# Sparse graph attention: sources projected ahead of targets, adjacency loaded from the start, gathers in memory of their own

## The reference

```python
hs = layer_norm(x); ht = layer_norm(h_target)            # masked by nodemask
q = (ht @ Wq + bq) / sqrt(32); k = hs @ Wk + bk; v = hs @ Wv + bv
logits = where(adj != 0, q . k, -1e30); probs = softmax(logits)     # per head
ht = layer_norm(ht + probs @ v @ Wo + bo); ff = gelu(ht @ W1) @ W2
out = layernorm(x + ht + ff)
```

## Time and profile before

| | us |
|---|---|
| median of 3 runs | 367.64 (366.29 to 369.21) |
| the profiled execution | 366.63 |
| its span | 364.8 |
| PE / DVE / ACT / POOL busy | 247.2 / 233.4 / 157.8 / 191.1 |
| mean granted clock of PE, of 1 | 0.867 |

### The profile page before, as it was taken

The page is one execution under the profiler, slowest core; times in us unless marked ns, Lnnn a source line. Parts: engine busy times, 40 slices in busy tenths (PEclk is TensorE's granted clock), DMA queues, the critical chain, the costliest instruction groups (busy, mean ns, idle before and its releaser), DMA issues. The chain is left out here.

```text
span 364.8 us, 4184 instructions
## 1 busy us (share of the span) xinstructions
PE 247.2 (68%) x1270; PEld 180.3 (49%) x1270; DVE 233.4 (64%) x648; ACT 157.8 (43%) x263; POOL 191.1 (52%) x209
## 2 busy tenths in 40 slices
PE   0339959897995020325999895879987979679900
PEld 0314413433431010215888785768876967578800
DVE  2613078989489854697798677767878679922110
ACT  0816403698766930002566652646534445223200
POOL 2699704325120037777778878887888712311210
PEclk9999967999999555555999998998999899969965
DMA  7993398999993017776765555555654610000000
GB/s 182 380 386 138 136 320 324 351 417 331 401 353 115 1 51 233 227 204 195 208 199 155 173 139 168 155 158 175 200 153 131 163 34 16 15 0 16 26 24 1
DMA packets 27972, 64.34 MB, mean 176 GB/s; under 512 B 6500, under 2 KB 14950, under 8 KB 25895
## 3 DMA queue, kind: packets, MB, share of 16 engines
q0 software_dynamic: 8368, 29.11, 27.5%
q1 hardware_dynamic: 11792, 25.44, 18.9%
q10 hardware_dynamic: 7782, 9.45, 7.3%
HBM read 53.50 MB, written 12.58 MB: 181 GB/s over the span
## 5 line engine op out<-in xcount | busy, mean ns | idle before, releaser
L610 POOL DMA_INDIRECT arena<-kv_scratch,places x79 | 92.8, 1175 | 22.7 <-issue 22.7
L797 PE MATMUL score<-h_t,w_sb 128*128 128x128 f32 x512 | 70.8, 298 | 7.3 <-ACT h_t L1073 7.2
L797 PEld LDWEIGHTS score<-h_t,w_sb 128*128 128x128 f32 x512 | 66.6, 211 | 10.6 <-ACT h_t L1073 10.6
L709 PE MATMUL bank<-arena 128*128 128x512 f32 x128 | 64.5, 643 | 10.8 <-POOLq L553 5.6
L806 PE MATMUL bank<-w_sb,gelu_t 128*128 128x256 f32 x256 | 58.3, 381 | 0.0
L806 PEld LDWEIGHTS bank<-w_sb,gelu_t 128*128 128x128 f32 x256 | 47.6, 190 | 7.9 <-ACT gelu_t L1049 1.9
L709 PEld LDWEIGHTS bank<-arena 128*128 128x128 f32 x128 | 25.6, 205 | 40.2 <-issue 39.0
L1359 DVE TENSOR_TENSOR arena<-arena,tab 128x1024 f32<-128x1024 f32 (+3 forms) x22 | 24.5, 1113 | 16.9 <-DMA arena<-kv_scratch,places 16.9
L627 POOL DMA_INDIRECT out_dram<-y_out,places x16 | 18.5, 1154 | 28.7 <-ACT y_out L1065 25.9
L606 POOL DMA_INDIRECT tab<-tab_scratch,places x16 | 15.6, 974 | 33.4 <-DVE place_value L1335 28.9
L991 ACT ACTIVATE gelu_t<-arena 128x2048 bf16<-128x2048 bf16 x16 | 30.6, 1910 | 3.8 <-issue 2.3
(11 more groups left out here) (127 smaller groups left out, 378.7 us busy)
## 6 DMA issues: line engine op xcount, KB each, us to landing
arena<-in_adj_dram SPq DMA_DIRECT2D x16, 1024.0 KB, 11.5
kv_scratch<-arena ACTq DMA_DIRECT2D x16, 256.0 KB, 5.5
tab_scratch<-arena ACTq DMA_DIRECT2D x16, 256.0 KB, 4.8
arena<-in_x_dram SPq DMA_DIRECT2D x4, 512.0 KB, 6.6
arena<-in_L_gnn_h_target_dram SPq DMA_DIRECT2D x4, 512.0 KB, 8.8
tab_scratch<-in_x_dram SPq DMA_DIRECT2D x1, 2048.0 KB, 13.8
w_sb<-in_L_gnn_W_dram SPq DMA_DIRECT2D x2, 1024.0 KB, 14.7
arena<-kv_scratch,places POOLq DMA_INDIRECT x79, 3.9
```

Of the source, the lines that this page charges most:

```text
L610: pool.indirect_dma_start(kv_ring[:, ring_at[m] + j, :], None, kv_dram[:, :], at).then_inc(gathered[m][piece], 16)
L709: mm = pe.matmul(proj_ps[n % 2], h_t[:, s, c % 2, k, i * P:(i + 1) * P], weights[:, k, :], start=(k == 0 and s == 0), stop=(k == DK - 1))
L797: mm = pe.matmul(hid_ps[2 * (n % 2) + half][:, f % 4 * P:(f % 4 + 1) * P], w1_sb[:, k, f * P:(f + 1) * P], h2_t[:, n % 2, k, :], start=(k ...
```

## The change

Work is arranged in eight units `(s, c)` in the order `UNITS`: sources 0 and 1, targets 0, sources 2 and 3, targets 1, 2, 3.

- **Adjacency**: SP loads tile 0 after the first two source chunks and interleaves the rest. The test moves to ACT for 12 of 16 tiles, as one activation `relu(1 - 1e7 * adj)` that also sums (`accum_out`); tiles 9, 11, 13 and 15 (`COMPARED`) are still compared on DVE and summed by `count` at the end of ACT's head.
- **PE**: two tiles of a unit, the transposes of the next unit, the other two tiles. `make_keys` 0, 1, 2 stand behind units 1, 3 and 4; `project_mean` and `make_keys(3)` stand in the middle of unit 6, so half of unit 6 and all of unit 7 come after them, and ahead of the sort's products, which now use the banks of `code_ps`.
- **DVE**: statistics, moves, picks and lists in a written order; statistics of unit 7 and tile 15 just before the last picks.
- **Stores**: two tiles at once (512 KB); `kv_out` gets 8 slots and its stores move to SP's queue; `tab_scratch` stores stay on ACT's.
- **POOL**: `key_rows` and `code_weights` first, the bias rows after them.
- **Memory**: sources' tokens, their transposes, weights and `key_rows` move to `tab`; edges and target work lie below slot 30 of `arena`; the gather ring starts at slot 30 (`RING_BEGIN`). The first gathers wait for the source stores and the mean row only; the first gather of target rows waits for `tab_scratch` and the copy of x; the first gather into slot 0 for the counts. A tile's first piece of edge rows is fetched before its target rows.
- **Flag**: `sum_tally` and `set_flag` move into the first steps of the second stage; `places` are clamped to N; `mlp_in(0)` waits for the flag.

```diff
@@ sync
+            load_x(0, 1)
...
+            load_adj(0)
+            sp.dma_start(wq_id[:, :, 0:D], Wq.rearrange("(k p) n -> p k n", p=P)).then_inc(wq_loaded, 16)
+            load_adj(1)
             load_x(1, 0)
...
+            load_adj(2)
+            load_adj(3)
+            load_x(0, 2)
+            load_adj(4)
+            load_x(0, 3)
+            save_kv(0, 0)
+            load_adj(5)
...
+            load_adj(8)
+            load_x(1, 2)
+            load_adj(9)
+            load_adj(10)
+            save_kv(2, 0)
...
+            load_adj(15)
+            load_x(1, 3)
             sp.dma_start(tab_dram[:, 2 * D:TAB], x[:, :]).then_inc(x_copied, 16)
@@ gpsimd
             pool.wait_ge(places_ready, 3)
-            pool.wait_ge(coded, QK * QUARTERS)
-            pool.wait_ge(counted, TILES)
-            pool.wait_ge(projected, 2 * TILES)
...
+            pool.wait_ge(v_added, TILES)
+            for r in range(KV_SLOTS // 2):
+                pool.wait_ge(kv_saved[r], 16 * CHUNKS // 2)
             pool.wait_ge(mean_saved, 16)
-            pool.wait_ge(x_copied, 16)
@@ tensor
+            turn_rows(0)
+            for u in range(len(UNITS)):
+                project(u, range(2))
+                if u + 1 < len(UNITS):
+                    turn_rows(u + 1)
+                if u == 6:
+                    project_mean()
+                    make_keys(3)
+                project(u, range(2, CT))
+                if u in (1, 3, 4):
+                    make_keys((1, 3, 4).index(u))
@@ scalar
+            def find_edges(t):
+                act.wait_ge(adj_loaded[t % AR], 16 * (t // AR + 1))
+                edges_free(act, t)
+                if t == QT:
+                    act.wait_ge(const_ready, 2)
+                act.activation(edges[:, t % ER, :], adj_sb[:, t % AR, :], ACT.Relu, bias=1.0, scale=-STEEP,
+                               accum_out=tally[:, 0, t:t + 1]).then_inc(edges_ready, 1)
...
+            normalise(0)
             act.wait_ge(ln_loaded, 16 * N_LN)
+            copy_turned(0)
+            normalise(1)
+            find_edges(0)
+            copy_turned(1)
+            find_edges(1)
+            normalise(2)
+            find_edges(2)
+            copy_turned(2)
+            find_edges(3)
+            normalise(3)
+            copy_projected(2, 0)
+            copy_projected(2, 1)
+            copy_turned(3)
+            save_projected(2, 0)
+            find_edges(4)
...
+            normalise(4)
+            copy_turned(4)
+            find_edges(6)
+            normalise(5)
+            find_edges(7)
+            copy_turned(5)
+            find_edges(8)
+            normalise(6)
+            find_edges(10)
...
+            find_edges(12)
+            normalise(7)
...
+            find_edges(14)
@@ vector
+            unit_stats(7)
+            compare(15)
+            pick_all(QUARTERS - 1)
+            split_keys(QUARTERS - 1)
+            list_edges(QUARTERS - 1)
```

More of the change, by code:

```diff
@@ L590, in _ @@
             pool.sem_inc(const_ready, 1)
-            for c in range(1, CHUNKS):
-                if c + 1 < CHUNKS:
-                    for s in range(2):
-                        rsqrt1(c + 1, s)
-                add_v(c)
+            rsqrt1(5)
+            add_v(2)
+            rsqrt1(6)
+            add_v(3)
+            rsqrt1(7)
             def fetch(m, j):
@@ L986, in count @@
-            def count(q):
-                for t in range(QT * q, QT * (q + 1)):
-                    act.wait_ge(edges_ready, t + 1)
-                    if t > 0:
-                        act.wait_ge(counted, t)
-                    act.activation(no_use, edges[:, t % ER, :], ACT.Identity, bias=0.0, scale=1.0,
-                                   accum_out=tally[:, 0, t:t + 1]).then_inc(counted, 1)
-            def load_w(dst, a):
-                act.dma_start(dst, a.rearrange("(k p) n -> p k n", p=P)).then_inc(weights_loaded, 16)
@@ new lines, in count @@
+            def count(t):
+                act.wait_ge(edges_compared, COMPARED.index(t) + 1)
+                if COMPARED.index(t):
+                    act.wait_ge(counted, COMPARED.index(t))
+                act.activation(no_use, edges[:, t % ER, :], ACT.Identity, bias=0.0, scale=1.0,
+                               accum_out=tally[:, 0, t:t + 1]).then_inc(counted, 1)
+            for dst, a in ((wkv[:, :, 0:D], Wk), (wkv[:, :, D:KV], Wv)):
+                act.dma_start(dst, a.rearrange("(k p) n -> p k n", p=P)).then_inc(wkv_loaded, 16)
@@ L1027, in _ @@
             act.dma_start(kv_dram[0:1, :], row_zero[:, :]).then_inc(mean_saved, 16)
-            count(QUARTERS - 1)
+            for half in range(2):
+                copy_projected(7, 2 * half)
+                copy_projected(7, 2 * half + 1)
+                save_projected(7, half)
+            for t in COMPARED:
+                count(t)
             def copy_context(n):
@@ new lines, in add_bias @@
+            def add_bias(u, some):
+                c = UNITS[u][1]
+                for i in some:
+                    t = CT * c + i
+                    dve.wait_ge(projected, CT * u + i + 1)
+                    if t >= KV_SLOTS:
+                        dve.wait_ge(kv_saved[kv_slot(t) // 2], 16 * (t // KV_SLOTS))
+                        dve.wait_ge(v_added, t - KV_SLOTS + 1)
+                    dve.scalar_tensor_tensor(out=kv_out[:, kv_slot(t), :], in0=proj_ps[i % 2], scalar=node[:, t:t + 1],
+                                             in1=bkv_bc, op0=ALU.mult, op1=ALU.add).then_inc(kv_read, 1)
```

569 lines of the change are left out of this document (301 added, 268 removed).

## The result

| | before | after |
|---|---|---|
| median, us | 366.97 (364.92 to 369.21, 4 runs) | 375.22 (373.95 to 376.16, 4 runs) |
| profiled execution / its span | 366.63 / 364.8 | 375.57 / 373.7 |
| mean granted clock of PE | 0.867 | 0.842 |
| first gather to last scatter | 217.7 | 219.7 |

The ratio is 1.022, with a 95% interval of 1.015 to 1.029. The forecast was 360.0 us with a range of 352 to 371.

The account below looks back on a forecast made before the run. The prediction took a serial head, then a second stage that moves with its first gather, as the bound. Layouts put the places at 124.1 instead of 130.7 us, 6.6 taken as 7, giving 360 us, range 352 to 371.

Parts of the forecast that it names:

- Start: Beginning of the head: PE starts projecting 10.7 us earlier than 24.27, then waits 2.9 us for POOL's bias rows.
- Now only Wk and Wv are wanted: Start of PE's projections: they need only these two weights, where before all weights and the bias rows came first.
- The sum: Head, old layout against new: places at 130.7 less 124.1 give 6.6 us, taken as 7 off the time.
- The loads' rival: Head: loads are the bound; at 300 GB/s the places move 13.6 us, to 373 us in all; chance 0.10.
- The bias rows: POOL in the head: they end at about 35.7, and the first target tile, wanted at 32.8, waits 2.9 us.
- The pass on ACT reading int32: Adjacency test on ACT: 2.0 us per pass, between bounds of 2.0 to 2.1 and 3.4.
- The first rival: ACT is the bound: passes of 2.6 us cancel the gain, 3.3 us give 376 us in all; chance 0.12.
- the table rival: ACT: Relu and Identity make it reload its table, 24 loads or 31 us, 390 us in all; chance 0.02.
- The middle: PE from 35.7 to make_keys(3): 43.9 us of work, but hand-overs with ACT put make_keys(3) at about 98 against 111.5.
- The end: After make_keys(3): the sort waits 5 us behind target projections; keys to places 25.5 us for 20.9, places at 124.1.
- The second stage: First gather to last scatter: stays 218 us, so a saving in the head is worth itself.
- The slower side: Whole kernel: chance 0.15 of being slower; among the rivals, ACT as bound had 0.12, loads 0.10, table 0.02.

Follow-up runs that it names:

- m1_mask_first: The changed kernel with the source mask's load issued first on ACT's queue instead of fifth: 363.86 us, ratio 0.985 to the kernel before.
- s1_sort_earlier: m1_mask_first with the last two target tiles on PE moved behind the sort's two rank products: 359.73 us, ratio 0.975; repeated on another chip 363.14 us, 0.970.
- x1_last_targets_earlier: s1_sort_earlier with the last target chunk's load moved on SP's queue from behind the last adjacency tile to ahead of tile 13: 361.95 us, ratio 0.952.
- p1_bias_round_early: s1_sort_earlier with POOL's first round of the bias rows moved ahead of rsqrt1(2): 361.02 us, ratio 0.959.
- the first two experiments: m1_mask_first (363.86 us), and the changed kernel with SP's first adjacency load waiting until the source mask, still fifth on ACT's queue, has landed (367.34 us).

## Why the prediction was wrong

It forecast 360.0 and the time is 375.22; the last write of the places, forecast at 124.1, came at 139.1.

- **The step that failed is "Start", "Now only Wk and Wv are wanted".** It holds for PE's first two tiles (13.33 us, forecast 13 to 14) and not for the third, since `add_bias` on DVE multiplies by the mask. The sum has no term for the mask's landing; loads stand in it by their bytes at 400 GB/s, and by that 8 KB cost nothing. Measured: 12.8 us of DVE and 9.7 us of PE, and the tiles behind it at a mean granted clock of 0.80 (30 to 40 us). m1_mask_first shows the cause itself: 7.5 us of the first gather come back.
- **Not all of the error was the mask.** The prediction's own landmarks, against the kernel after and the two with the mask first, us:

| | forecast | after | m1_mask_first | s1_sort_earlier |
|---|---|---|---|---|
| first target tile | 35.7 | 48.74 | 38.45 | 38.27 |
| keys 1 | 58 | 73.94 | 63.54 | 60.61 |
| keys 2 | 75 | 89.89 | 79.44 | 76.42 |
| keys 3 | 98 | 114.86 | 106.14 | 103.58 |
| last write of the places | 124.1 | 139.1 | 131.6 | 123.8 |

  At the first target tile the kernel after is 13.0 us late and m1_mask_first 2.8: the mask is some 10 us there, and the 2.8 left go, as far as the timeline tells, to the biases that its new place delays and to the first target chunk (DVE waits for them until 17.1 and until 18.5). Then m1_mask_first loses the 2.9 us of the lower clock, which s1_sort_earlier doesn't. Between keys 2 and 3 both lose 3.0 to 3.5 us on the forecast's 23.7, and with the last target chunk's load earlier x1_last_targets_earlier takes 23.5, so that load is the term. s1_sort_earlier meets the forecast of the places by luck and not by the forecast's path: it is 5.6 us late at keys 3 and has the sort's wait taken out.
- **The loads' rival was looked for in the wrong place.** It asked whether bandwidth would run short, and gave as its sign windows under 330 GB/s with PE idle before 90 us. The sign came: from 20 to 30 us the window shows 311 GB/s and PE busy 0.61 us. But with the mask moved the same window shows 400 GB/s and PE busy 8.58, so memory had more to give. The harm came from one queue's packets standing between another's. The last target chunk was the second such term: it is last in SP's order, DVE waited 2.9 us for it (4.5 with the mask first), and the prediction had no line for it.
- **The bias rows**: forecast 2.9 us, measured 2.83. Right, and also right that all of PE stands behind it: p1_bias_round_early gets 2.5 us back.
- **The pass on ACT reading int32**: forecast 2.0, measured 1.912 and 0.201 for the accumulator, 12 times; one table load in the head, at 3.4 us. The groups of the first 140 us after:

```profile
L1084 ACT ACTIVATE arena<-arena 128x2048 bf16<-128x2048 int32 x12 | 22.9, 1912 | 1.0 <-ACT arena L1070 1.0
...
L1084 ACT ACTIVATION_READ_ACCUMULATOR arena<-arena 128x1 f32 x12 | 2.4, 201 | 0.0
L1051 ACT ACT_TABLE_LOAD x1 | 1.3, 1283 | 3.4 <-issue 3.4
```

  The line through copies of 256 and 512 columns gave it. The first rival (a dearer pass) and the table rival are out. The Trainium skill's rule that relu belongs on VectorE ("ScalarE: Activation LUTs", section "Rules for kernel authors") didn't decide this change, as the counting pass was ACT's already. Its direction agrees with the trace, where a compare on DVE takes 1.2 to 1.3 us.
- **The middle**: PE's waits ahead of keys 1, 2, 3 forecast 4.0, 4.0, 3.4, measured 3.95, 3.90, 3.03. Right.
- **The end**: the sort waits 5 us behind target tiles forecast, 5.4 measured, and s1_sort_earlier shows that it was a matter of order. Class product to the last write of the places: 8.6 forecast, 8.6 measured (130.50 to 139.14). The prediction's text has two ends for the old kernel, 132.1 for the row numbers and 132.4 for the last write; the sum used the second.
- **The second stage**: forecast unchanged. 219.7 against 217.7, and 216.7 in both of the first two experiments, which share all its code: not a cost of the change that these runs could show.
- **The slower side** had been given mostly to ACT, with 0.12. The right rival for that side would have been: a small load is late, and every engine that waits for its semaphore with it.

## What to carry to other kernels

When loads are moved ahead, list for each engine which semaphore it waits on first and every load that counts into it; `bkv_loaded` at 48 stood for three loads, the last of them made of 2048 pieces. Issue loads of small pieces before any queue begins to stream large rows, and look at what they push back: here the biases landed 7 us later for it. Loading the mask in whole rows would be another way, which no run here tried. And read an edit in the middle of a chain from the landmark ahead of it to the one behind it: what an execution lost before that point, to the clock above all, would otherwise be put down to the edit.

## What was not expected of the hardware

- One load of 8 KB in pieces of 4 bytes took 5.6, 8.1, 9.9, 14.0 or 23.4 us, by what the other queue carried meanwhile: mostly rows of 1 KB in the first three, two adjacency tiles of 8 KB rows in the fourth, a stream of them in the last.
- The same 2.8 us wait of PE was followed by the lower clock, for 6.8 us from 37.2 on, in one execution and by no change in another of the same instructions; the first lost 2.9 us by the next key block.
- The same kernel's second stage took 217.1 us in an execution on one chip and 224.3 in one on another, while its head agreed within 0.5 us. In the second the 20 us from 164 had POOL busy 10.35 of 20 and PE's clock at 0.85, against 16.09 and 1.00 in the first. About half of the 7.2 us is the choice of execution: the first was 1.7 us faster than its kernel's median and the second 1.7 slower. Why the rest, isn't settled.
